# Two routed expert layers on one Trainium2 core: TensorE's steps written out, each step's expert read once

## The chip, the cores and the metric

The kernel runs on one core of one Trainium2 chip, as one program. The metric is device time in microseconds (us) of one execution. Times and the profile below are of the kernel before the change.

## The reference, cut to what matters

The reference is a stack of four blocks, each an attention-like layer and a feed-forward layer added to a residual `x` of 2048 tokens by 512. Two of its eight layers are routed, and the change touches only these:

```python
# gated layer (third block): 8 experts, 2 for each token, inner width 352
routing_weights = softmax(x @ gate_w.T); topk_w, topk_i = top_k(routing_weights, 2)
topk_w = topk_w / sum(topk_w)
for e in range(8):
    w_e = sum(where(topk_i == e, topk_w, 0.0), axis=-1)
    gated = silu(x @ w_gate[e]) * (x @ w_up[e])
    out = out + w_e[:, None] * (gated @ w_down[e])
# last layer (fourth block): 16 routed experts, 2 for each token, inner width 256
rt_mid = gelu(einsum('th,ehd->ted', xt, Wrt_up))
routed_out = einsum('ted,edh->th', rt_mid * gate[:, :, None], Wrt_down)
```

The last layer has two shared experts as well, which another part of the kernel computes.

## The kernel before, in words

The program is a sequence of blocks, one behind the other; the five engines meet at the end of each. A router block gives every token two slots. Slots are sorted by expert and padded so that 128 of them, a step, belong to one expert: 39 steps in the gated layer, 47 in the last. For each step there is an expert number in `step_expert` and, in `step_token`, the token of each of its slots. Which expert a step has is known only at run time.

`routed_block` (from L473) is called for both layers. All experts' weights are kept in on-chip memory, each split into two 16-bit halves (`up16`, `dn16`, high and low), and every product is made of three passes: high by high, low by high, high by low. A step `s` runs so:

- GpSimd (L613) copies the step's token numbers (`cur`) and gathers their rows into `g`, which has two buffers; the gather of step s + 2 waits for the transposes of step s (`g_T`).
- TensorE transposes the 128 rows, 4 transposes (`rows_transposed`, L647); ScalarE makes their high half (`y_high`, L714), VectorE the low half (`y_low`, L773).
- TensorE multiplies by the expert's up weights (`up`, L655): 3 passes of 4, or of 8 in the gated layer, matmuls. ScalarE and, in the gated layer, VectorE apply the activation (`first_half`, L727, `second_half`, L787).
- TensorE transposes the middle (`middle_transposed`, L665; 2 or 3 transposes), the two engines split it (`middle_high`, L736, `middle_low`, L793), and TensorE multiplies by the down weights (`down`, L673): 6 matmuls in the last layer, 9 in the gated one.
- ScalarE evicts the result (`results`, L742), and SyncE stores it (L582). After all steps each token's two results are gathered, scaled and added to `x`.

TensorE's steps overlap (L687): in step s it first reads the expert of s and that of s - 1, then transposes the rows of s + 1, runs the first up pass of s, transposes the middle of s - 1, runs the other two up passes, and last the down matmuls of s - 1.

The weights' matmul operands are addressed by the expert's register (`bass.ds(e, 1)`), so a register operation stands ahead of each up and down matmul. `expert_of` (L644) reads one number from on-chip memory into a register of TensorE's queue, with a lower and an upper bound, which makes the queue check the value.

All engines run their steps through `run_steps` (L519): the first 8 or 16 steps are written out, and in them (`filling`) the weights arrive, two experts ahead, through a staging tile of 3 or 5 pieces (SyncE L569, ScalarE L720, VectorE L778). Then comes a loop of two steps a turn, 14 turns, steps 8 to 35 in the gated layer and 16 to 43 in the last; then three written-out steps. In the loop a step's number is a register, so every wait that counts steps is against a computed value.

Of the kernel before, what the change touches and what calls it, by code (L numbers as in the profile page):

```python
# [44 lines left out]
class Env:  # L45
# [6 lines left out]
    def sem(self, name):  # L52
        self.names += 1
        handle = self.live.enter_context(self.nc.semaphore(f"{name}_{self.names}"))
        self.sems.append(handle)
        return handle
# [416 lines left out]
def routed_block(nc, env, rows, slots_out, w_up, w_down, kind, inner, routing, final, n_exp, first_expert):  # L473
# [4 lines left out]
    gates, slot, step_expert, step_token = routing  # L478
    NS = step_expert.shape[1]
# [3 lines left out]
    NC, full, rest = len(chunks), inner // P, inner % P  # L483
# [8 lines left out]
    with ExitStack() as ctx:  # L492
# [20 lines left out]
        hi_done, lo_done, padded = sem("mid_hi"), sem("mid_lo"), sem("mid_pad")  # L513
# [5 lines left out]
        def run_steps(engine, step):  # L519

            for s in range(n_exp):
                step(s, s % 2)
            with engine.Fori(n_exp // 2, (NS - TAIL) // 2) as i:
                step(i * 2, 0)
                step(i * 2 + 1, 1)
            for s in range((NS - TAIL) // 2 * 2, NS):
                step(s, s % 2)

        def from_step(s, n):

            return not isinstance(s, int) or s >= n

        def before_end(s, n):

            return not isinstance(s, int) or s + n < NS

        def filling(s):
            return isinstance(s, int) and s < n_exp

        def turns(s, w):  # L540

            return s + (2 - w)
# [21 lines left out]
        def pieces_split(q):  # L564

            return sum(operations(p % NPC) for p in range(q + 1))
# [75 lines left out]
        @block.tensor  # L642
        def _(pe):
            def expert_of(s):  # L644
                return pe.value_load(step_expert[0:1, bass.ds(s, 1)], min_val=0, max_val=n_exp - 1)

            def rows_transposed(s, w):  # L647
                pe.wait_ge(g_in[w], 8 * turns(s, w))
                if from_step(s, 1):
                    pe.wait_ge(yl_done, s)  # L650
                for k in range(KD):
                    last = nc.tensor.transpose(pT[:, k, :], g[:, w, k * P:(k + 1) * P], env.id32[:])  # L652
                last.then_inc(g_T, 1)

            def up(s, w, e, some):  # L655
                for i in some:
                    a, h = passes[i]
                    for k in range(KD):
                        for j in range(n_up):
                            last = nc.tensor.matmul(pu[w][:, j, 0:inner], y16[a][:, w, k, :], up16[h][:, bass.ds(e, 1), j, k, :],  # L660
                                                    start=(i == 0 and k == 0), stop=(i == 2 and k == KD - 1))
                if some[-1] == 2:
                    last.then_inc(up_done, 1)

            def middle_transposed(s, w):  # L665
                pe.wait_ge(mid_done, s + 1)
                if from_step(s, 1):
                    pe.wait_ge(lo_done, s)
                for c in range(NC):
                    last = nc.tensor.transpose(pM[:, c, :], mid[:, w, c * P:(c + 1) * P], env.id32[:])  # L670
                last.then_inc(mid_T, 1)

            def down(s, w, e):  # L673
                if filling(s):
                    pe.wait_ge(w_ready, pieces_split(s * NPC + n_up))
                if from_step(s, 2):
                    pe.wait_ge(o_done, s - 1)
                pe.wait_ge(lo_done, s + 1)
                i = 0
                for c, n in enumerate(chunks):  # L680
                    for a, b in passes:
                        last = nc.tensor.matmul(po[w][:], mid16[a][0:n, w, c, :], dn16[b][0:n, bass.ds(e, 1), c, :],  # L682
                                                start=(i == 0), stop=(i == len(passes) * NC - 1))
                        i += 1
                last.then_inc(dn_done, 1)

            def step(s, w):  # L687
                e = expert_of(s)
                before = expert_of(s - 1) if from_step(s, 1) else None
                if before_end(s, 1):  # L690
                    rows_transposed(s + 1, 1 - w)
                if filling(s):
                    pe.wait_ge(w_ready, pieces_split(s * NPC + n_up - 1))
                pe.wait_ge(yl_done, s + 1)
                if from_step(s, 2):
                    pe.wait_ge(mid_done, s - 1)
                up(s, w, e, (0,))
                if from_step(s, 1):
                    middle_transposed(s - 1, 1 - w)
                up(s, w, e, (1, 2))  # L700
                if from_step(s, 1):
                    down(s - 1, 1 - w, before)
            if rest:
                pe.wait_ge(padded, 1)
            rows_transposed(0, 0)
            run_steps(pe, step)
            s = NS - 1
            e = expert_of(s)
            middle_transposed(s, s % 2)
            down(s, s % 2, e)  # L710

        @block.scalar
        def _(act):
# [2994 lines left out]
```

## Time and profile before

| | us |
|---|---|
| three runs | 3191.45, 3192.67 (median), 3192.72 |
| the profiled execution | 3193.02 |
| its span, first to last instruction | 3191.3 |
| TensorE busy (matmuls) | 2408.4 (75%) |
| VectorE busy | 2057.9 (64%) |
| ScalarE busy | 1507.0 (47%) |
| GpSimd busy | 1076.2 (34%) |

The shares are those of the whole program, of which the two routed layers' steps are some 530 us: 1779 to 2077 us from the span's start for the gated layer, 2895 to 3136 us for the last. In the rows, PE is TensorE, PEld its weight loads, DVE VectorE, ACT ScalarE, POOL GpSimd, SP SyncE; a name with a q (PEldq) is the engine's instruction queue, whose instructions are not counted as busy. `L652` is a line of the kernel before, and `mo_yT<-ident,mo_g` says what an instruction writes and reads: `mo_yT` are transposed rows, `mo_pu` up products, `mo_mid` the middle, `mo_midT` the middle transposed, `mo_po` down products, `mo_o` the evicted result.

### The profile page before, as it was taken

The numbers are of one execution on the slowest core, as the hardware profiler recorded it, in microseconds if no ns is written. First come the engines' busy times: TensorE is split into PE (matmuls) and PEld (weight loads), VectorE is DVE, ScalarE is ACT, GpSimd is POOL, SyncE is SP. The second block draws the span as 40 slices with busy tenths as digits, with TensorE's granted clock in tenths as the row PEclk, the third lists the DMA queues.
The fourth block names the chain that finished last, engine by engine and source line by source line (L and its number), as shares of the span: only waits on it lengthen the run. The fifth ranks groups of instructions, "written<-read, shape, count | busy, mean of one in ns | idle before, by whom it ended". The sixth has DMA issues, their size and how long they took to land. (4 is left out here: it accounts for less than half of the span.)

```text
span 3191.3 us, 40561 instructions
## 1 busy us (share of the span) xinstructions
PE 2408.4 (75%) x13100; PEld 1072.8 (34%) x13101; DVE 2057.9 (64%) x3302; ACT 1507.0 (47%) x2076; POOL 1076.2 (34%) x818
## 2 busy tenths in 40 slices
PE   2987998899969925676675589909888887996772
PEld 1541332444434302222222355505422222444441
DVE  6656775445456898999996632256588886656313
ACT  2543554254332755555552443325477776335432
POOL 5775766011001235666662111155621000002224
PEclk9987999899979958899896799959799999998996
DMA  4642220220000000000001632254602100307435
GB/s 153 197 156 70 83 84 30 94 86 1 1 4 12 1 0 1 0 0 0 0 0 54 201 125 72 69 165 165 231 28 80 67 15 24 100 24 253 140 102 184
DMA packets 128394, 245.29 MB, mean 77 GB/s; under 512 B 32515, under 2 KB 59407, under 8 KB 126310
## 3 DMA queue, kind: packets, MB, share of 16 engines
q1 hardware_dynamic: 107094, 169.49, 15.1%
q0 software_dynamic: 21136, 73.68, 7.6%
q8 instruction: 96, 1.57, 0.2%
q14 instruction: 68, 0.56, 0.1%
HBM read 154.24 MB, written 88.60 MB: 76 GB/s over the span
## 5 line engine op out<-in xcount | busy, mean ns | idle before, releaser
L1895 DVE TENSOR_REDUCE ac_nmax<-ac_M 128x1 f32<-128x512 f32 (+1 forms) x768 | 491.8, 677 | 93.6 <-PE ac_M L1728 89.4
L1877 ACT ACTIVATE ac_PT<-ac_S 128x1024 f32<-128x1024 f32 x384 | 388.7, 1022 | 206.2 <-PE ac_S L1755 169.5
L3471 POOL TENSOR_TENSOR sc_hc<-sc_h,sc_cs 128x1024 f32<-128x1024 f32 x128 | 300.8, 2357 | 156.9 <-DVE sc_h L3586 93.5
L3586 DVE TENSOR_TENSOR_SCAN sc_h<-sc_dA,sc_dB 128x1024 f32<-128x1024 f32 x128 | 292.1, 2282 | 12.3 <-ACT sc_dA L3552 12.3
L3506 PE MATMUL sc_y<-sc_hc,ident 128*128 128x512 f32 x512 | 257.9, 631 | 18.6 <-DVE x_res L3602 16.3
L775 DVE SCALAR_TENSOR_TENSOR mo_y16l<-mo_yT,mo_y16h 128x512 f16<-128x512 f32 x86 | 59.4, 691 | 241.7 <-ACT mo_y16h L718 241.7
L3552 ACT ACTIVATE sc_dA<-ss_delta,sc_A 128x511 f32<-128x511 f32 x256 | 166.0, 682 | 28.6 <-DVE sc_h L3586 27.8
L3484 PE MATMUL sc_b<-ss_bc,sc_sel 128*128 128x512 f16 x128 | 53.5, 418 | 154.0 <-DVE sc_dB L3578 122.5
L3578 DVE TENSOR_TENSOR sc_dB<-ss_du,sc_b 128x1024 f32<-128x1024 f32 x128 | 156.1, 1220 | 17.7 <-PE sc_b L3484 7.1
L3557 ACT ACTIVATE sc_cs<-sc_c 128x512 f32<-128x512 f32 x128 | 76.2, 596 | 185.4 <-POOL sc_hc L3471 182.4
L1728 PE MATMUL ac_M<-KT,QT 64*128 64x512 f16 (+1 forms) x384 | 134.5, 425 | 33.2 <-DVE ac_nmax L1895 17.2
L3506 PEld LDWEIGHTS sc_y<-sc_hc,ident 128*128 128x128 f32 x512 | 102.6, 202 | 111.6 <-issue 73.1
L1774 PE MATMUL ac_o<-ac_PT,ac_V 128*32 128x512 f32 x1024 | 138.7, 614 | 0.3 <-ACT ac_oT L1853 0.2
L1728 PE MATMUL ac_M<-ac_KT,ac_QT 64*128 64x512 f16 (+1 forms) x384 | 117.5, 386 | 25.8 <-DVE ac_nmax L1895 19.7
L1208 PE MATMUL ap_t<-ident,ap_y 128*128 128x128 f32 x128 | 20.4, 284 | 135.0 <-DVE ap_y L1396 135.0
L652 PE MATMUL mo_yT<-ident,mo_g 128*128 128x128 f32 x344 | 57.1, 290 | 85.5 <-issue 60.1
L1755 PE MATMUL ac_S<-QT,KT 64*128 64x512 f16 (+1 forms) x384 | 103.9, 393 | 19.4 <-ACT ac_PT L1877 19.4
L618 POOL COPY mo_cur<-step_token_last 128x1 int32 (+1 forms) x47 | 9.8, 208 | 313.4 <-POOLq L72 177.3
L718 ACT ACTIVATE mo_y16h<-mo_yT 128x512 f16<-128x512 f32 x86 | 51.2, 595 | 126.5 <-PE mo_yT L652 126.4
L2795 DVE SCALAR_TENSOR_TENSOR f_midl<-f_mid,f_midh 128x512 f16<-128x512 f32 x64 | 54.6, 860 | 82.1 <-ACT f_midh L2728 82.1
L1655 POOL TENSOR_TENSOR ac_psum<-ac_PT 128x1024 f32<-128x1024 f32 x32 | 74.8, 2359 | 82.1 <-PE ac_M L1799 81.9
L1755 PE MATMUL ac_S<-ac_QT,ac_KT 64*128 64x512 f16 (+1 forms) x384 | 99.0, 383 | 2.0 <-ACT ac_PT L1877 1.9
(623 smaller groups left out, 5754.0 us busy)
## 6 DMA issues: line engine op xcount, KB each, us to landing
keys_t<-ap_kto SPq DMA_DIRECT2D x32, 512.0 KB, 2.6
queries_t<-ap_qto SPq DMA_DIRECT2D x32, 512.0 KB, 2.7
slot_results_last<-mo_o SPq DMA_DIRECT2D x47, 256.0 KB
slot_results<-mo_o SPq DMA_DIRECT2D x39, 256.0 KB
values<-ap_vf SPq DMA_DIRECT2D x32, 256.0 KB, 2.9
ac_KT<-keys_t POOLq DMA_DIRECT2D x4, 2048.0 KB, 8.4
ac_QT<-queries_t POOLq DMA_DIRECT2D x16, 512.0 KB, 10.3
attended<-ac_A SPq DMA_DIRECT2D x8, 1024.0 KB, 3.8
```

The source lines that it names most:

```text
L1655: g.tensor_tensor(psum3[:, p], first, PT[:, n % PTB], ALU.add).then_inc(p_added, 1)
L1728: nc.tensor.matmul(psM[:, slot, :], QT[b % 2][base:base + n, c, j * P:(j + 1) * P], KT[b % 2][base:base + n, :, c, :], start=True, stop=Tr ...
L1755: last = nc.tensor.matmul(psS[:, 2 * (n % 2) + i, :], KT[b % 2][base:base + k, kt, c, :], QT[b % 2][base:base + k, c, :], start=True, stop ...
L1774: last = nc.tensor.matmul(po[r * VC:(r + 1) * VC, :], V[b % 2][:, kt, g % NG * GH + r, :], PT[:, m % PTB, i, :], start=(kt == 0), stop=(kt ...
L1877: nc.scalar.activation(PT[:, n % PTB, :, :], psS[:, 2 * (n % 2):2 * (n % 2) + 2, :], ACT.Exp, scale=SCALE / (SQK * SQK)).then_inc(exp_done, 1)
L1895: last = v.tensor_reduce(out[:, :, 0], sc[:, 0:MAIN], AX.X, ALU.max)
L3471: nc.gpsimd.tensor_tensor(hc[:, m % RC, :, :], h[:, m % RH, :, :], cs[:, m % 2, :].unsqueeze(1).to_broadcast([P, W, S]), ALU.mult).then_in ...
L3506: last = nc.tensor.matmul(py[:, c, :], env.id32[:], hc[:, m % RC, c, :], start=(n == 0), stop=(n == NS - 1))
L3552: last = nc.scalar.activation(dA[:, m % 2, c, 1:S], delta[:, b * KD + k, 1:S], ACT.Exp, scale=A[:, k, n:n + 1])
L3557: nc.scalar.activation(cs[:, m % 2, :], pc[:], ACT.Copy).then_inc(c_ev, 1)
L3578: nc.vector.tensor_tensor(dB[:, m % RB, :, :], chans(du, b, p), pb[:].unsqueeze(1).to_broadcast([P, W, S]), ALU.mult).then_inc(dB_done, 1)
L3586: nc.vector.tensor_tensor_scan(h[:, m % RH, :, :].rearrange("p c s -> p (c s)"), dA[:, m % 2, :, :].rearrange("p c s -> p (c s)"), dB[:, m ...
```

## The change

Only TensorE's part of `routed_block` changes. Its steps are no longer run through `run_steps` but written out, all 39 or 47, so that every wait is against a constant and there is no branch. The expert of a step is read once, behind the down matmuls that end the preceding step, and carried over as `before` for the next; the read has no bounds. The other engines keep their loops.

```diff
             def expert_of(s):
-                return pe.value_load(step_expert[0:1, bass.ds(s, 1)], min_val=0, max_val=n_exp - 1)
+                return pe.value_load(step_expert[0:1, s:s + 1])
...
-            def step(s, w):
-                e = expert_of(s)
-                before = expert_of(s - 1) if from_step(s, 1) else None
-                if before_end(s, 1):
+            if rest:
+                pe.wait_ge(padded, 1)
+            rows_transposed(0, 0)
+            e, before = expert_of(0), None
+            for s in range(NS):
+                w = s % 2
+                if s + 1 < NS:
                     rows_transposed(s + 1, 1 - w)
                 if filling(s):
                     pe.wait_ge(w_ready, pieces_split(s * NPC + n_up - 1))
                 pe.wait_ge(yl_done, s + 1)
-                if from_step(s, 2):
+                if s >= 2:
                     pe.wait_ge(mid_done, s - 1)
                 up(s, w, e, (0,))
-                if from_step(s, 1):
+                if s:
                     middle_transposed(s - 1, 1 - w)
                 up(s, w, e, (1, 2))
-                if from_step(s, 1):
+                if s:
                     down(s - 1, 1 - w, before)
-            if rest:
-                pe.wait_ge(padded, 1)
-            rows_transposed(0, 0)
-            run_steps(pe, step)
-            s = NS - 1
-            e = expert_of(s)
-            middle_transposed(s, s % 2)
-            down(s, s % 2, e)
+                if s + 1 < NS:
+                    e, before = expert_of(s + 1), e
+            middle_transposed(NS - 1, w)
+            down(NS - 1, w, e)
```

## Rows read from the trace of the kernel before

**Rows 1.** Windows: gated layer's loop, last layer's loop, nine of its filling steps.

```profile
core 0: us, PE busy (x) PEld busy (x) DVE busy (x) ACT busy (x) POOL busy (x), PEclk, DMA share, GB/s
1860.56:2058.57 198.01, 182.10 (x1121) 111.24 (x1121) 49.69 (x84) 59.82 (x112) 32.28 (x56) 1.00 0.23 74
2974.45:3120.00 145.55, 106.34 (x672) 64.20 (x673) 28.64 (x56) 54.96 (x112) 32.56 (x56) 1.00 0.31 101
2917.44:2959.78 42.34, 33.22 (x217) 21.07 (x217) 31.20 (x37) 33.67 (x54) 10.46 (x18) 1.00 0.98 332
```

**Rows 2.** Waits of PE (us, times, longest): gated loop, last loop, gated filling.

```profile
PE mo_yT L652 <- issue: 16.6, 29, 0.8
...
PE mo_yT L652 <- issue: 32.8, 28, 1.4
...
PE mo_pu L660 <- DVE mo_up16l L784: 14.1, 7, 5.6
```

**Rows 3.** Timeline (start, us), last layer's loop: first and last down matmul, next transposes.

```profile
2992.50 0.39 PE L682 MATMUL mo_po<-mo_dn16h,mo_mid16h 128*128 x1 [0.26 <-DVE mo_mid16l L795]
...
2993.59 0.38 PE L682 MATMUL mo_po<-mo_dn16l,mo_mid16h 128*128 x1
...
2995.33 0.65 PE L652 MATMUL mo_yT<-ident,mo_g 128*128 128x128 f32 x4 [1.37 <-issue]
```

**Rows 4.** Lines L645 and L660 on PE's queue: ns min/median/max, first and last start.

```profile
L645 PEldq SEQ_ASSERT  x172: 18/18/24, 1780.3 to 3132.9; - x172
L645 PEldq TENSOR_LOAD <-step_expert_last x94: 294/300/314, 2895.3 to 3132.3; - x94
...
L660 PEldq FUSED_REGOPS  x1500: 51/55/65, 1785.7 to 3131.1; - x188
```

**Rows 5.** Timeline, PE: a written-out step of the last layer, and the next one's start.

```profile
2945.68 0.63 PE L652 MATMUL mo_yT<-ident,mo_g 128*128 128x128 f32 x4 [0.67 <-issue]
...
2948.25 0.39 PE L682 MATMUL mo_po<-mo_dn16h,mo_mid16h 128*128 x1 [0.33 <-DVE mo_mid16l L795]
...
2949.34 0.38 PE L682 MATMUL mo_po<-mo_dn16l,mo_mid16h 128*128 x1
2950.37 0.63 PE L652 MATMUL mo_yT<-ident,mo_g 128*128 128x128 f32 x4 [0.66 <-issue]
```

**Rows 6.** Line L645 in the turn of that step, 2948.8 to 2950.3.

```profile
L645 PEldq TENSOR_LOAD <-step_expert_last x2: 297/298/300, 2948.9 to 2949.6; - x2
```

**Rows 7.** Timeline, PE: a written-out step behind the gated layer's loop.

```profile
2058.57 0.63 PE L652 MATMUL mo_yT<-ident,mo_g 128*128 128x128 f32 x4 [0.30 <-issue]
...
2064.67 0.38 PE L682 MATMUL mo_po<-mo_dn16l,mo_mid16h 96*128 x1
2065.10 0.63 PE L652 MATMUL mo_yT<-ident,mo_g 128*128 128x128 f32 x4
```

**Rows 8.** DMA issues in the gated layer's loop: the gather, us to landing.

```profile
mo_g<-normalised,mo_cur POOLq DMA_INDIRECT x28, 3.3
```

**Rows 9.** Timeline, ACT and DVE, in the loop step of rows 3.

```profile
2990.70 0.60 ACT L718 ACTIVATE mo_y16h<-mo_yT 128x512 f16<-128x512 f32 x1 [1.10 <-PE mo_yT L652]
...
2994.00 0.60 ACT L745 ACTIVATE mo_o<-mo_po 128x512 f32<-128x512 f32 x1 [1.26 <-PE mo_po L682]
...
2991.33 0.69 DVE L775 SCALAR_TENSOR_TENSOR mo_y16l<-mo_yT,mo_y16h 128x512 f16<-128x512 f32 x1 [3.98 <-ACT mo_y16h L718]
2991.93 0.41 DVE L795 SCALAR_TENSOR_TENSOR mo_mid16l<-mo_midT,mo_mid16h 128x256 f16<-128x256 f32 x1
```

**Rows 10.** Timeline of a filling step of the last layer.

```profile
2961.68 0.41 DVE L795 SCALAR_TENSOR_TENSOR mo_mid16l<-mo_midT,mo_mid16h 128x256 f16<-128x256 f32 x1
...
2962.35 0.39 PE L682 MATMUL mo_po<-mo_dn16h,mo_mid16h 128*128 x1 [0.36 <-DVE mo_mid16l L795]
```

**Rows 11.** DMA queues, packets and MB: gated loop 1860.56:2058.57, last filling 2908.01:2969.20.

```profile
q8 instruction: 1, 0.02, 0.0%
...
q8 instruction: 4, 0.07, 0.4%
```

## The prediction

> **What bounds the kernel now.** I read the windows by stage first. The change touches only the two routed layers, and of these the two loops are the bulk: 198.01 us for the 28 loop steps of the gated layer (steps 8 to 35), 7.07 us a step, and 145.55 us for the 28 of the last layer (steps 16 to 43), 5.20 us a step [rows 1]. TensorE is busy for 182.10 and 106.34 us of them, at the full granted clock (1.00), while VectorE, ScalarE and GpSimd are each busy for well under half: TensorE's own order of work sets the step, and the clock is no issue.
>
> The waits of TensorE come next. In both loops the one large idle stands before the row transposes that open a step, and it ends by "issue", that is, by nothing that another engine did: 16.6 us in the gated layer, 32.8 us in the last [rows 2]. The third row is of another kind: while the gated layer fills its weights, TensorE waits for VectorE's weight split (14.1 us).
>
> The timeline shows one such turn. The last down matmul starts at 2993.59, the next transposes at 2995.33: 1.74 us, where matmuls that follow one another without a gap start 0.22 us apart [rows 3]. What TensorE's queue does meanwhile is told by the line of the expert's read: 172 assertions for 86 steps, two reads a step, each of some 0.30 us [rows 4].
>
> The kernel also holds a sample of what the change makes. Steps that are not in the loop already have constant waits, and still read twice. In the last layer such a step takes 2945.68 to 2950.37 = 4.69 us, against 5.20 in the loop, and its turn 2949.34 to 2950.37 = 1.03 us [rows 5]. In that turn the two reads begin at 2948.9 and 2949.6 [rows 6]: a read with its bounds check holds the queue for 0.7 us, and the first starts 0.4 us before the last down matmul does, so the queue runs ahead of the array. In the gated layer the one clean turn between two such steps is 2064.67 to 2065.10 = 0.43 us, and the step 2058.57 to 2065.10 = 6.53 us [rows 7].
>
> **Part 1, constant waits and no branch.** This removes the register arithmetic of the waits, the loop's count and branch, and the address arithmetic of each read. Taken alone it is worth the step's difference in the sample: 7.07 - 6.53 = 0.54 us and 5.20 - 4.69 = 0.51 us a step.
>
> **Part 2, one read less, and no bounds check on the other.** Place in the order: the read stood at the start of a step, right behind the preceding down matmuls; now it stands at the end of that step, right behind the same matmuls. Nothing is moved past anything, and no DMA, wait or semaphore changes place. A read without a check does not occur in the trace. From below it costs its load alone, 0.29 us; from above it costs what a checked read does, 0.7 us [rows 4, 6]. I take no value, because both ends are hidden. In the gated layer even 0.7 us less than a turn of 0.43 us is below the 0.22 us that the array needs anyway. In the last layer a checked read that begins at 2948.9 lets the transposes start near 2949.7, where the array is free at 2949.34 + 0.22 = 2949.56; the remaining 0.1 us meets the next bound, below.
>
> **What is late next, gated layer.** With a full queue the step is TensorE's own stream: 2058.57 to 2064.67 plus 0.22 = 6.32 us [rows 7]. ScalarE is busy for 59.82 / 28 = 2.1 us of a step, VectorE for 1.8, and gathered rows land 3.3 us after their issue with two steps' time to do so [rows 1, 8]. Gain 7.07 - 6.32 = 0.75 us a step, 21.0 us for 28, and 0.75 us for the turn into the loop and 0.2 us for the last turn: 22.0 us.
>
> **What is late next, last layer.** Six down matmuls leave less cover. TensorE alone would need 0.22 + (2948.25 - 2945.68) + (2949.34 - 2948.25) = 3.88 us [rows 5]. But ScalarE first evicts the down result, then the transposed rows, and the next down matmuls need both halves of the middle, which come behind the rows' halves on both engines. Around that ring: last down start to result eviction 2994.00 - 2993.59 = 0.41; eviction 0.60; rows' high half to rows' low half 0.63; low half to the middle's low half 0.60; from there to the first down matmul 0.67 in a constant step (0.57 in the loop); first to last down matmul 1.09 [rows 3, 9, 10]. Together 4.00 us, 0.12 us longer than TensorE's own. I take 4.00; the ends are 3.88, and 4.69 if nothing of the read comes free. Gain 1.20 us a step: 33.6 us for 28, 1.2 us for the turn into the loop, and two steps behind the loop at 4.69 - 4.00 each, 1.4 us. Together 36.2 us.
>
> **What is gained nothing, or little.** The gated layer's eight filling steps wait for weights (14.1 us before the up matmuls [rows 2]); a shorter turn only lengthens that wait: 0. If this cover were gone, 7 turns of 0.5 us would be worth 3.5 us. The last layer's filling steps do not wait for weights, but the DMA engines are busy for 0.98 of the time at 332 GB/s [rows 1], 4.70 us a step for nine steps. A step's bytes at a share of 1 need 0.98 x 4.70 = 4.61 us: 0.09 us a step, 1.2 us for 13.
>
> **New cost: straight-line code.** TensorE's 28 looped steps a layer are now fetched. In the filling steps, already written out, 4 instruction blocks came in 61.19 us (13 steps), with the other engines' fetches among them, while the DMA engines were full, and the constant step above still took 4.69 us; the gated layer's loop brought 1 block in 198 us [rows 11]. So about 28 / 13 x 4 = 9 more blocks in the last layer and, with 40 matmuls a step in place of 24, 14 in the gated one, 23 in all. From below 0 each; from above, as the mean of nine filling steps (4.70) lies 0.01 us above the single step, 0.01 x 13 / 4 = 0.03 us each, 1 us in all. I take 0. A page of the Trainium skill bears on this (Runtime: NRT & Kernel Launch, "Instruction fetch mechanics"): code streams in by 16 KiB blocks which the sequencer fetches while it runs the current one, mostly hidden. By that rule the sum is the same and rival 4 below has next to no chance; the trace agrees as far as it goes, with 4 blocks at an unchanged pace.
>
> **Sum.** 22.0 + 36.2 + 1.2 = 59.4 us against the profiled execution's own 3193.02 us (span 3191.3): 3133.6, so **3134 us**. The median of the runs shown, 3192.67, is 0.35 us below that execution, which changes nothing.
>
> **The rivals.**
> 1. *The turn stays as it is in the constant steps* (the remaining read, or the load's answer, is what the array waits for). For it: every constant turn of the last layer is still 1 us long. Against it: its two reads follow one another, 0.7 us apart. Gain 28 x 0.54 + 28 x 0.51 = 29.4, about 1 us for the turns into the loops: 3163 us. Chance 0.08.
> 2. *The last layer's filling steps follow to 4.00 us as well*, because the full DMA engines carry slack that no row shows. Another 13 x 0.70 - 1.2 = 7.9 us: 3126 us. Against it the share of 0.98. Chance 0.06.
> 3. *The address arithmetic takes it back.* Each up and down matmul is preceded by a register operation of 55 ns [rows 4] on the expert's register, 33 a step in the gated layer and 18 in the last. Should a register without known bounds need two where one did, a step's queue gets 1.8 and 1.0 us longer, which eats the gain: about 3192 us. Nothing in the trace speaks for it but that it is not shown. Chance 0.04.
> 4. *Slower: the fetch of the written-out code stalls TensorE.* Place: each block boundary in the two former loops, 23 of them. It decides from 59.4 / 23 = 2.6 us a block on; at 4 us, 92 us are added to 3134: 3226 us. For it: the loop hardly fetches at all. Against it: the filling steps, though they are only 13. Chance 0.04.
>
> That the diff does not remove the second read can hardly be; rival 1 would be its time.
>
> **How the numbers follow.** The forecast has 0.78. Two runs of this kernel can be told apart from about 0.2%, 6 us, on. Faster by more: 0.78 + 0.08 + 0.06 = 0.92; within: 0.04; slower: 0.04. The range: the unknowns of the forecast itself are the last layer's step (3.88 gives 3.4 us more gain; 4.3, half way to the constant step, costs 8.4) and the gated filling (3.5 more); with rival 2 that is 3123 below. Above I go to 3150, which takes in a last layer at 4.4 and a gated step 0.2 us over its stream; rivals 1, 3 and 4, together 0.16, stay outside.
>
> **What would show it.** Right: one read a step and no assertion; turns of 0.22 us in the gated layer, steps of 6.3 us; steps of 4.0 us in the last layer, with TensorE's wait moved to the middle's low half before the down matmuls, and ScalarE's row eviction following its result eviction without idle. Filling steps hardly changed, with the DMA share at 1. Wrong: an "issue" idle that stays before the row transposes (rival 1), longer gaps between up matmuls (rival 3), single steps with idle of microseconds at a regular distance (rival 4).

## The result, and the profile after

The changed kernel takes 3657.98 us (median of 4 runs, 3656.35 to 3659.91), the kernel before 3192.66 us (4 runs); the ratio is 1.146 (95% interval 1.144 to 1.148). It was forecast to become 1.8% faster and is 14.6% slower. The profiled execution after has a span of 3656.7 us, 465.4 us more than before.

Where the time went is seen by stage. Windows of the changed kernel over the same steps as [rows 1]: the gated layer's former loop (28 steps), the last layer's (28 steps), and the middle of the last layer's filling.

```profile
core 0: us, PE busy (x) PEld busy (x) DVE busy (x) ACT busy (x) POOL busy (x), PEclk, DMA share, GB/s
1904.81:2326.42 421.61, 359.86 (x1121) 113.36 (x1121) 49.67 (x84) 60.19 (x113) 32.27 (x56) 0.82 0.11 36
3330.17:3570.68 240.51, 201.00 (x673) 75.30 (x673) 31.26 (x56) 54.94 (x112) 32.55 (x56) 0.76 0.20 62
3251.00:3310.00 59.00, 48.81 (x167) 18.55 (x166) 24.98 (x28) 25.95 (x41) 8.14 (x14) 0.78 0.55 180
```

The gated step went from 7.07 to 421.61 / 28 = 15.06 us, the last layer's from 5.20 to 8.59 us. The matmuls are as many as before (1121 and 673), and the other engines did the same work in the same busy time. TensorE's busy time about doubled, with its clock at 0.82 and 0.76 in place of 1.00. The filling steps do not shelter from it either: the DMA share fell from 0.98 to 0.55, so the weights no longer set the pace there.

The waits of TensorE in the two windows (total us, times, longest), against the 16.6 and 32.8 us of [rows 2]:

```profile
PE mo_pu L660 <- issue: 6.0, 29, 0.3
```

```profile
PE mo_pu L660 <- issue: 9.3, 48, 0.3
```

The wait before the row transposes (L652), which the change was to remove, is gone, and nothing of its size took its place. This is a trap. By waits and busy time the engine now looks 85% busy (359.86 of 421.61) and hardly idle. But a matmul is counted from its start to its modelled end, and many small gaps are hidden between such overlapping entries. The starts tell more. Timeline (start, us) of the end of one gated step of the changed kernel, the last up pass (8 matmuls), four of the nine down matmuls, and the next step's transposes:

```profile
2198.49 3.44 PE L660 MATMUL mo_pu<-mo_up16l,mo_y16h 128*128 x8
2202.01 0.61 PE L682 MATMUL mo_po<-mo_dn16h,mo_mid16h 128*128 x1
2202.43 0.62 PE L682 MATMUL mo_po<-mo_dn16h,mo_mid16l 128*128 x1
2202.84 0.63 PE L682 MATMUL mo_po<-mo_dn16l,mo_mid16h 128*128 x1
...
2205.54 0.40 PE L682 MATMUL mo_po<-mo_dn16l,mo_mid16h 96*128 x1
2206.03 0.52 PE L652 MATMUL mo_yT<-ident,mo_g 128*128 128x128 f32 x3
```

Down matmuls start 0.42 us apart, and the eight up matmuls ahead of them (2202.01 - 2198.49) / 8 = 0.44 us. Before, down matmuls started 0.22 us apart [rows 3], and the up matmuls of a gated step (2062.94 - 2061.75) / 8 = 0.15 us. Timeline of the kernel before:

```profile
2061.75 1.36 PE L660 MATMUL mo_pu<-mo_up16l,mo_y16h 128*128 x8
2062.94 0.38 PE L682 MATMUL mo_po<-mo_dn16h,mo_mid16h 128*128 x1
```

One rival has to go first. Most of that stretch of the changed kernel ran at half the clock (0.50 in the first window below), where by estimate a down matmul alone takes the array twice 0.22 us. But the last down matmuls of the next step ran at a clock of 1.00 (second window), and they still start 0.42 us apart:

```profile
2199.00:2205.00 6.00, 5.92 (x15) 1.41 (x15) 0.52 (x1) 0.46 (x1) 0.00 (x0) 0.50 0.00 0
2219.50:2221.00 1.50, 1.32 (x4) 0.29 (x3) 0.00 (x0) 0.04 (x1) 0.00 (x0) 1.00 0.00 0
```

```profile
2219.70 0.39 PE L682 MATMUL mo_po<-mo_dn16h,mo_mid16h 96*128 x1
2220.11 0.39 PE L682 MATMUL mo_po<-mo_dn16h,mo_mid16l 96*128 x1
2220.53 0.39 PE L682 MATMUL mo_po<-mo_dn16l,mo_mid16h 96*128 x1
```

So the clock does not make the gaps. It does make the entries longer (0.63 against 0.39 us), which is one more reason why TensorE looks busy. What lies between the matmuls stands on TensorE's queue. The lines of the expert's read (L645), of the up matmuls (L660) and of the down matmuls (L682) in the changed kernel (ns min/median/max, first and last start, against [rows 4]):

```profile
L645 PEldq TENSOR_LOAD <-step_expert_last x47: 296/301/311, 3191.9 to 3587.3; - x47
...
L660 PEldq FUSED_REGOPS  x3000: 51/106/165, 1785.4 to 3593.0; - x188
L660 PEldq SEQ_ASSERT  x1500: 18/18/28, 1785.6 to 3592.9; - x188
...
  issue: 477.8, 1477
...
L682 PEldq SEQ_ASSERT  x633: 18/18/18, 1810.4 to 3600.3; - x159
```

The read has indeed become one a step, without an assertion. But its check did not vanish: it moved to every place where the value is used. Each of the 1500 up matmuls and 633 down matmuls has two register operations and an assertion ahead of it, where it had one register operation. There were 172 assertions, there are 2133 now. The idle time before the up matmuls, by this view, is 477.8 us in 1477 pieces.

### The profile page after: what moved, and what is told of

It reads as the page before. It is cut to its first block and busy times, and to the rows that moved or that the text cites. A ratio compares the mean times of both kernels' runs of the same rounds, so it can differ in the third digit from the quotient of the medians.

```text
span 3656.7 us, 44002 instructions
## 1 busy us (share of the span) xinstructions
PE 2812.1 (77%) x13100; PEld 1090.6 (30%) x13100; DVE 2062.1 (56%) x3302; ACT 1508.9 (41%) x2076; POOL 1071.0 (29%) x818
## 5 line engine op out<-in xcount | busy, mean ns | idle before, releaser
L774 DVE SCALAR_TENSOR_TENSOR mo_y16l<-mo_yT,mo_y16h 128x512 f16<-128x512 f32 x86 | 59.4, 691 | 385.8 <-ACT mo_y16h L717 385.5
L660 PE MATMUL mo_pu<-mo_up16l,mo_y16h 128*128 x500 | 179.7, 371 | 43.9 <-issue 9.7
L660 PE MATMUL mo_pu<-mo_up16h,mo_y16l 128*128 x500 | 155.6, 315 | 48.0 <-issue 7.9
L660 PE MATMUL mo_pu<-mo_up16h,mo_y16h 128*128 x500 | 156.4, 333 | 44.7 <-issue 6.9
L618 POOL COPY mo_cur<-step_token_third 128x1 int32 (+1 forms) x39 | 8.9, 228 | 492.3 <-PE mo_yT L652 463.8
L789 DVE SCALAR_TENSOR_TENSOR mo_mid<-mo_pu,mo_mid 128x352 f32<-128x352 f32 x39 | 20.5, 525 | 228.0 <-ACT mo_mid L731 228.0
L744 ACT ACTIVATE mo_o<-mo_po 128x512 f32<-128x512 f32 x86 | 51.4, 597 | 227.6 <-PE mo_po L682 227.6
L1727 PE MATMUL ac_M<-ac_KT,ac_QT 64*128 64x512 f16 (+1 forms) x384 | 117.5, 386 | 25.9 <-DVE ac_nmax L1894 19.8
L682 PE MATMUL mo_po<-mo_dn16h,mo_mid16h 128*128 (+1 forms) x211 | 121.6, 576 | 15.8 <-issue 7.8
```

Source lines behind the costliest of these rows:

```text
L1727: nc.tensor.matmul(psM[:, slot, :], QT[b % 2][base:base + n, c, j * P:(j + 1) * P], KT[b % 2][base:base + n, :, c, :], start=True, stop=Tr ...
```

## The experiments

The theory (A): without declared bounds the queue checks the register at each use, and this sets the pace. The rival (B): the written-out code is slow by itself, by its fetch. A third (C): some of both. The first four kernels ran together, the last two together, each beside the kernel before (3192.9 and 3192.8 us).

**The changed kernel with the bounds put back on its one read.**

```diff
-                return pe.value_load(step_expert[0:1, s:s + 1])
+                return pe.value_load(step_expert[0:1, s:s + 1], min_val=0, max_val=n_exp - 1)
```

> The changed kernel with the bounds put back on its one read for each step (lower 0, upper the last expert); all else stays: steps written out, constant waits, one read. Theory A (the missing bounds put a check ahead of each of the 2133 up and down matmuls, and that is the whole loss): checks fall from 2133 to 86, steps become 6.3 us in the gated layer and about 4.0 us in the last, and the time is that of the prediction, 3134 us (3123 to 3150). Rival B (the written-out code itself is slow, through its fetch or its length): still above 3550 us. Rival C (the two share the loss): between 3200 and 3500 us.

Measured: 3132.04 us (5 runs), ratio 0.981 (0.980 to 0.982). So the missing bounds cost all of the slowdown, 526 us, and the forecast of 3134 us holds for this kernel. Its windows: both former loops, and the last layer's fourteen filling steps.

```profile
1861.03:2037.15 176.12, 176.12 (x1122) 113.45 (x1121) 49.66 (x84) 58.07 (x112) 32.21 (x56) 1.00 0.27 85
2946.40:3061.77 115.37, 102.54 (x674) 65.70 (x673) 28.60 (x56) 54.98 (x112) 32.48 (x56) 1.00 0.40 129
2886.63:2946.40 59.77, 51.20 (x338) 32.94 (x337) 46.56 (x55) 50.52 (x82) 17.78 (x28) 1.00 0.94 332
```

In the gated layer TensorE is busy for 176.12 of 176.12 us, 6.29 us a step, with the clock back at 1.00. The lines of the read and of the up matmuls of this kernel show where the check now is, 86 times, and that one register operation is left ahead of each matmul:

```profile
L645 PEldq FUSED_REGOPS  x86: 151/151/165, 1780.0 to 3069.4; - x86
L645 PEldq SEQ_ASSERT  x86: 18/18/28, 1780.3 to 3069.6; - x86
```

```profile
L660 PEldq FUSED_REGOPS  x1500: 51/55/60, 1785.7 to 3071.5; - x188
```

**The kernel before with only its bounds taken off**, loop and two reads kept.

```diff
-                return pe.value_load(step_expert[0:1, bass.ds(s, 1)], min_val=0, max_val=n_exp - 1)
+                return pe.value_load(step_expert[0:1, bass.ds(s, 1)])
```

> The kernel before, its loop and its two reads for each step kept, with nothing but the bounds taken off the read. Theory A: a check ahead of every up and down matmul in the loop too, steps of some 15 us and 8.6 us (a little more than in the changed kernel, because the second read and the branch are still there), 3650 to 3700 us. Rival B: the loop is as fast as before, 3185 to 3195 us, since only written-out code is slow.

Measured: 3731.96 us (one run). The loop suffers as much as the written-out steps; with the same 1500 and 633 assertions its steps take 449.92 / 28 = 16.07 and 270.58 / 28 = 9.66 us in its windows:

```profile
1909.61:2359.53 449.92, 385.97 (x1120) 120.39 (x1121) 49.65 (x84) 60.20 (x112) 32.20 (x56) 0.71 0.10 33
3372.59:3643.17 270.58, 224.54 (x673) 74.25 (x673) 31.25 (x56) 54.78 (x112) 32.48 (x56) 0.62 0.17 54
```

B and C fall: this kernel is the slowest of all, with 102 instruction blocks fetched where the kernel before has 96. The time is above what A expected. A step is 1.0 us longer here than in the changed kernel in both layers, more than the 0.54 and 0.51 us that I had put on the constant waits. A likely reason, which no run isolates, is that where the queue sets the pace, everything that stands on it counts in full, the second read too.

**Bounds declared, and no check anywhere.** The read's value is told to lie within 0 and the last expert, with the check at the read left out as well.

```diff
-                return pe.value_load(step_expert[0:1, s:s + 1])
+                return nc.s_assert_within(pe.value_load(step_expert[0:1, s:s + 1]), 0, n_exp - 1,
+                                          skip_runtime_bounds_check_because="the router writes no other number")
```

> The changed kernel with the bounds declared for the value read and no check made of them anywhere: 0 checks. Theory A, as the prediction put it: a read's own check (0.2 to 0.3 us) is hidden in the gated layer and all but 0.1 us of it in the last, so the time is that of the run with the bounds put back, less 0 to 5 us: 3128 to 3134 us. Rival (the read's own check still shows in every turn): 15 to 25 us under the run with the bounds put back.

Measured: 3125.22 us (5 runs), ratio 0.979 (0.978 to 0.980), the fastest of all. It is 6.8 us below the kernel with one checked read, slightly over the range given. The gated step stays at 176.12 us for 28; the last layer's comes to 109.97 / 28 = 3.93 us, 0.19 below 4.12. The timeline of one such step (first and last down matmul, next transposes; lines past the read stand one lower in this kernel) against [rows 3] and [rows 5]:

```profile
3005.25 0.39 PE L683 MATMUL mo_po<-mo_dn16h,mo_mid16h 128*128 x1 [0.46 <-DVE mo_mid16l L795]
...
3006.34 0.38 PE L683 MATMUL mo_po<-mo_dn16l,mo_mid16h 128*128 x1
3006.55 0.60 PE L653 MATMUL mo_yT<-ident,mo_g 128*128 128x128 f32 x4
```

The turn is 0.21 us, the array's own pace. With one checked read it is still 3004.01 - 3003.63 = 0.38 us (timeline of the kernel with the bounds put back):

```profile
3003.63 0.38 PE L682 MATMUL mo_po<-mo_dn16l,mo_mid16h 128*128 x1
3004.01 0.63 PE L652 MATMUL mo_yT<-ident,mo_g 128*128 128x128 f32 x4
```

**Constant waits, but both checked reads at the start of a step.** Of the written-out kernel, this undoes the one read.

```diff
-                return pe.value_load(step_expert[0:1, s:s + 1])
+                return pe.value_load(step_expert[0:1, s:s + 1], min_val=0, max_val=n_exp - 1)
...
-            e, before = expert_of(0), None
             for s in range(NS):
                 w = s % 2
+                e, before = expert_of(s), expert_of(s - 1) if s else None
...
-                if s + 1 < NS:
-                    e, before = expert_of(s + 1), e
```

> Written-out steps with constant waits, but two checked reads at the start of each step, as the kernel before has them: the first part of the change alone. By the prediction's first part and its rival 1: 0.54 us a step in the gated layer and 0.51 us in the last, 3163 us (3155 to 3170); the rest of the way to 3134 us is then the second read's. Rival B: above 3550 us.

Measured: 3160.83 us (4 runs), ratio 0.990 (0.989 to 0.992). Constant waits alone are thus worth 32 us, the second read another 29 us (3132.04), and the check of the remaining read 6.8 us. The total is near the 3163 us expected, but the steps are not: in the windows of the two former loops a gated step gains (198.01 - 178.80) / 28 = 0.69 us where 0.54 was expected, a step of the last layer (145.55 - 134.01) / 28 = 0.41 us where 0.51 was. The two misses nearly cancel.

```profile
1857.60:2036.40 178.80, 178.64 (x1121) 111.49 (x1121) 49.62 (x84) 59.13 (x112) 32.15 (x56) 1.00 0.27 83
2953.46:3087.47 134.01, 103.29 (x673) 65.43 (x673) 28.62 (x56) 54.87 (x112) 32.42 (x56) 1.00 0.34 110
```

**Half way: the up matmuls with a register read with bounds, the down matmuls with a second one read without.**

```diff
             def expert_of(s):
-                return pe.value_load(step_expert[0:1, s:s + 1])
+                return pe.value_load(step_expert[0:1, s:s + 1], min_val=0, max_val=n_exp - 1)
+
+            def expert_unbounded(s):
+                return pe.value_load(step_expert[0:1, s:s + 1])
...
-            e, before = expert_of(0), None
+            e, free, before = expert_of(0), expert_unbounded(0), None
...
-                    e, before = expert_of(s + 1), e
+                    e, free, before = expert_of(s + 1), expert_unbounded(s + 1), free
...
-            down(NS - 1, w, e)
+            down(NS - 1, w, free)
```

> The changed kernel with two reads a step: the up matmuls use a register read with bounds, the down matmuls one read without. So 633 of the 2133 addressed matmuls keep the check ahead of them. Theory A, put in numbers: a step lasts as long as the longer of two things, TensorE's own stream (6.3 and 3.9 us) and its queue's work. The queue's work: 0.42 us for each checked matmul, 0.13 us for each other matmul or transpose, 0.7 us for the bounded read and 0.3 for the other. Gated layer: 9 x 0.42 + 31 x 0.13 + 1.0 = 8.8 us; last layer 6 x 0.42 + 18 x 0.13 + 1.0 = 5.9 us. With 31 and 47 steps that is 3132 + 78 + 78 = 3288 us at most, and near 3240 if a read overlaps (8.0 and 5.3 us). Up matmuls keep their pace of 0.22 us, down matmuls start 0.42 us apart. Rival D: a register without bounds slows the queue whatever its uses; the up matmuls slow down as well and the time stays within 100 us of the changed kernel's 3658.

Measured: 3331.12 us (4 runs), ratio 1.044 (1.042 to 1.046). The cost follows the uses, so D falls. Lines of the up matmuls (L663, in 0.75 us of one step) and of the down matmuls (L685, in the step before it) of this kernel:

```profile
L663 PEldq FUSED_REGOPS  x6: 55/55/55, 1911.0 to 1911.7; - x6
```

```profile
L685 PEldq FUSED_REGOPS  x18: 46/106/151, 1905.6 to 1909.2; - x18
L685 PEldq SEQ_ASSERT  x9: 18/18/18, 1905.8 to 1909.2; - x9
```

In these two neighbouring steps, both at a granted clock of 1.00, the queue puts out an unchecked up matmul every 0.7 / 5 = 0.14 us and a checked down matmul every 3.4 / 8 = 0.43 us. The first is the array's own pace for up matmuls (0.15 us above), so 0.14 us is the most that an unchecked one costs the queue; the second is twice what the array needs (0.22 us). The time is still 43 us above the upper estimate, and the steps say why. Two gated steps one after the other:

```profile
1910.49:1919.33 8.84, 7.81 (x41) 3.96 (x41) 1.77 (x3) 2.15 (x4) 1.15 (x2) 1.00 0.19 61
1919.33:1929.58 10.25, 9.12 (x40) 4.79 (x41) 1.77 (x3) 2.15 (x4) 1.15 (x2) 0.83 0.17 53
```

At the full clock a step takes 8.5 to 8.8 us, near the 8.8 of the estimate; where the clock was low for part of the step, 10.25. By the timeline that holds for 15 of the 28 steps of the former loop, at some 1.4 us each, 21 us. The last layer kept its clock at 1.00, but its steps took 6.24 us where 5.9 was estimated: 47 x 0.34 = 16 us.

**The loop and both reads, bounds declared and no check at the read.**

```diff
-                return pe.value_load(step_expert[0:1, bass.ds(s, 1)], min_val=0, max_val=n_exp - 1)
+                return nc.s_assert_within(pe.value_load(step_expert[0:1, bass.ds(s, 1)]), 0, n_exp - 1,
+                                          skip_runtime_bounds_check_because="the router writes no other number")
```

> The kernel before, loop and two reads a step and all, its reads declared to lie within 0 and 15 (7 in the gated layer) without a check at the read. It tells how much of the loop's turn were the reads' own checks, and how much the waits and addresses that count steps. If a check costs 0.19 us a read, as between the two kernels that are written out with bounds, two reads give 0.4 us a step: 28 x 2 x 0.4 = 22 us, 3170 us. If it costs 0.4 us a read (a checked read held the queue 0.7 us, its load 0.3): 28 x 2 x 0.7 (no more than what keeps the turn above the array's) = 39 us, 3154 us. Rival: the checks were the turn, and the loop comes to within 10 us of the written-out kernel's 3125.

Measured: 3151.53 us (4 runs), ratio 0.987 (0.985 to 0.989). The time is near the second of the two estimates, but not for its reason. That estimate put the whole gain into the loops, at 0.7 us a step. The loops' windows give (198.01 - 181.86) / 28 = 0.58 us a step in the gated layer and (145.55 - 129.39) / 28 = 0.58 us in the last, 32 us in all, and the other 9 us lie in the written-out steps, which the estimate left out. A read's check is thus worth 0.29 us while the turn is long, not 0.4.

```profile
1858.25:2040.11 181.86, 179.40 (x1121) 111.31 (x1122) 49.68 (x84) 59.29 (x112) 32.28 (x56) 1.00 0.25 81
2952.87:3082.26 129.39, 106.67 (x672) 64.25 (x673) 28.63 (x56) 54.72 (x113) 32.56 (x56) 1.00 0.35 113
```

The rest of the turn, 26 us against the written-out kernel without checks, is, by what differs between the two kernels, the second load, the waits and addresses that count steps, and the branch. In its last-layer loop TensorE still waits at the turn, half of the 32.8 us of before:

```profile
PE mo_yT L653 <- issue: 16.5, 28, 0.9
```

So a single line in the kernel before, its loop untouched, gives three fifths of what the whole rewriting could give (41 of 68 us).

## Why the prediction was wrong

**The step that failed** is in Part 2, "one read less, and no bounds check on the other". It took the check to be a piece of the read, which goes when the bounds go, and bounded the read's own price on both sides. The bounds are what lets the kernel go without checks at the matmuls; taken away, they bring 2133 checks where there were 172. Rival 3 had the right place, the register operations ahead of each up and down matmul, and even the form, "need two where one did". Its price was wrong: I took the second operation at the 55 ns of the first. It takes 151 ns, an assertion follows, and the queue's pace goes from at most 0.14 to 0.43 us a matmul. That is at least 33 x 0.29 = 9.6 us a gated step where I had 1.8. The sign that I had named for this rival, longer gaps between up matmuls, is what came: 0.44 us in place of 0.15. The array's 6.3 us no longer cover it: 33 x 0.42 = 13.9 us, and a read, seven transposes and the waits make 15.06.

That rival's price was bounded by the nearest row only in kind (a register operation), not in purpose. The row of the same purpose stood in [rows 6]: a checked read holds the queue 0.7 us, its load 0.3, so a check is worth up to 0.4 us. By this row the rival would have added 33 x 0.4 = 13 us of queue to a gated step, twice the array's 6.3 us: the right sign and the right order of size, far above the range's 3150.

**Point by point**, with the bounds put back:
- Part 1, constant waits, and rival 1's number 3163: 3160.83 with two reads, by two misses that nearly cancel (0.69 for 0.54 us in the gated layer, 0.41 for 0.51 in the last).
- Gated step 6.32: 6.29, no idle left. Gain 28 x 0.78 = 21.9, forecast 21.0 for the loop.
- Last layer's step 4.00: 4.12 with the checked read, 3.93 without one. The named next wait came: TensorE waits for the middle's low half before the down matmuls, 28 times, 12.5 us in the loop of the kernel with one checked read:

```profile
PE mo_po L682 <- DVE mo_mid16l L794: 12.5, 28, 0.5
```

- But with one checked read the ring through ScalarE's result eviction is not the bound: ScalarE evicts a result at 3004.05 and again at 3008.16, each for 0.60 us, and starts on the rows only at 3004.75 and 3008.99, the second time with a wait for TensorE's transposes:

```profile
3008.99 0.60 ACT L717 ACTIVATE mo_y16h<-mo_yT 128x512 f16<-128x512 f32 x1 [0.23 <-PE mo_yT L652]
```

  The chain that closes there is TensorE's own: transposes, halves, middle's low half, down matmuls, next transposes. Without any check ScalarE does go from the result to the rows without idle, as foreseen, but 0.52 us after the eviction's start (2998.90 to 2999.42) where the ring had 0.60. With that term the ring adds up to the measured 3.93 us, as TensorE's chain does too; which of them binds in that kernel is not shown. So, with one checked read, what the turn loses is lost in full, and "both ends are hidden" was wrong by 0.19 us a step.
- The last layer's filling, "4.61 us at a share of 1": 59.77 / 14 = 4.27 us. The nine steps of [rows 1] moved 332 GB/s x 42.34 us = 14.1 MB, 1.56 MB a step, so the transfers ran ahead of the steps there; all fourteen need 332 x 59.77 = 19.8 MB, 1.42 MB a step. I took the bytes of a stretch for the bytes of its steps. Rival 2 was thus half right, and the gain here is 14 x 0.48 = 6.7 us, not 1.2.
- Gated filling 0: 9.15 us a step against 9.07 over its last six steps, as forecast.
- Straight-line code: 19 more instruction blocks over the whole program than before, 23 estimated, at a gated step of 6.29 us without idle. Rows of the instruction queue on the pages of before, of the kernel with the bounds put back, and of the changed one:

```profile
q8 instruction: 96, 1.57, 0.2%
```

```profile
q8 instruction: 115, 1.88, 0.3%
```

```profile
q8 instruction: 131, 2.15, 0.2%
```

  Rival 4 had the sign but not the cause. The Trainium skill (Runtime: NRT & Kernel Launch, "Instruction fetch mechanics") calls the crossing of a block mostly hidden; the trace agrees, with 28 gated steps of 6.29 us each.

The sum of 59.4 us met 60.6 us (3192.67 - 3132.04), with 3.4 us too much in the last layer's loop and 5.5 too little in its filling. That the total came so close is luck in part, two misses of opposite sign. The kernel that it met still checks its one read; the one that matches the forecast's terms, one read and no check anywhere, takes 3125.22 us, inside the range. The forecast was right for a kernel that was not in the diff.

## What to carry to other kernels

In these runs a register that addresses an operand carries its bounds with it: where they are not declared, the check is paid at each use, so declare them once at the read, and where the values are known to be good, declare them unchecked. When a diff takes a safeguard away, ask who relied on it, and price the rival by the row of the same purpose. And when a queue is suspected, look at the starts of neighbouring instructions and at the queue's own lines, not at busy shares and waits.

## What the runs showed of the hardware

A check of a register against its bounds is a register operation of 151 ns with an assertion of 18 ns. With the address operation of 55 ns, and gaps that no view here names, it spaces addressed matmuls 0.42 to 0.44 us apart on TensorE's queue, at a clock of 0.50 and of 1.00 alike. Without it up matmuls of the gated layer come every 0.14 us, as fast as the array takes them. Ahead of a read, where the turn is long, a check costs 0.29 us.

I had not expected the clock to follow. In the kernels with the check at every use TensorE's granted clock falls to between 0.62 and 0.82 in the two loops, part of the time at 1.2 GHz; with the check at the down matmuls alone it is 0.90 in the gated loop; in all other loop windows it is 1.00, 2.4 GHz. Before the falls the array had been doing matmuls spaced by its queue. Where the queue sets the pace this costs nothing. Two neighbouring gated steps of the changed kernel:

```profile
2191.01:2206.03 15.02, 13.37 (x41) 4.35 (x41) 1.77 (x3) 2.20 (x5) 1.15 (x2) 0.74 0.10 36
2206.03:2221.05 15.02, 12.48 (x40) 3.95 (x41) 1.77 (x3) 2.19 (x5) 1.15 (x2) 0.89 0.10 35
```

The clock is 0.74 in one and 0.89 in the other, the time is 15.02 us in both. Where only the down matmuls are checked it does cost: 10.25 against 8.84 us above. The Trainium skill (TensorE: Matmul & The Clock Gate, Part 1) says that the gate's ratio follows how busy the array has been; these windows agree in direction (1121 matmuls of the gated loop in 421.61 us at 0.82, 1122 in 176.12 us at 1.00), and no run here sets the clock by itself.
